# First attention of a two-layer kernel: every product on tiles of 64 rows and 32 columns

## The reference, cut to what matters

```python
qkv = zn @ w_qkv
qkv5 = qkv.reshape(b, n, H, HD, 3)
...
scores = jnp.einsum('bhqd,bhkd->bhqk', q, k) / SCALING
att = jax.nn.softmax(scores, axis=-1)
out = jnp.einsum('bhal,bhlv->bhav', att, v)
```

## Time and profile before

| | us |
|---|---|
| median of 3 runs | 1337.25 (1336.49 to 1337.75) |
| the profiled execution | 1338.72, span of its instructions 1336.7 |
| first attention, within the span | from 115.6 to about 780 |
| mean granted clock of TensorE | 0.955 |

### The profile page before, as it was taken

The page is one execution under the profiler, slowest core; times in us unless marked ns, Lnnn a source line. Parts: engine busy times, 40 slices in busy tenths (PEclk is TensorE's granted clock), DMA queues, the critical chain, the costliest instruction groups (busy, mean ns, idle before and its releaser), DMA issues. The chain is left out here.

```text
span 1336.7 us, 32111 instructions
## 1 busy us (share of the span) xinstructions
PE 1210.5 (91%) x13377; PEld 609.2 (46%) x13377; DVE 1007.4 (75%) x1288; ACT 837.6 (63%) x1447; POOL 238.0 (18%) x309
## 2 busy tenths in 40 slices
PE   6967999999999999999999978898899899899980
PEld 4641222232222223222322335555699566688870
DVE  6878999999999999999999547765675688533324
ACT  3543888888888888888888855565222466533331
POOL 4200110000000000000000011100573222145560
PEclk9986999999999999999999989998998699999995
DMA  5764133232233322323321121100010211223317
GB/s 146 200 206 91 30 65 75 45 78 62 61 79 75 76 59 63 81 45 74 68 51 75 57 69 44 39 17 16 19 44 28 68 37 37 60 72 99 101 50 191
DMA packets 75228, 95.35 MB, mean 71 GB/s; under 512 B 13236, under 2 KB 44684, under 8 KB 74052
## 3 DMA queue, kind: packets, MB, share of 16 engines
q1 hardware_dynamic: 69996, 83.19, 24.5%
q0 software_dynamic: 5088, 10.12, 2.5%
HBM read 54.30 MB, written 38.56 MB: 69 GB/s over the span
## 5 line engine op out<-in xcount | busy, mean ns | idle before, releaser
L613 DVE TENSOR_REDUCE b_mx<-psum 128x2 f32<-128x1024 f32 x507 | 595.6, 1218 | 38.8 <-PE psum L558 35.6
L671 ACT ACTIVATE b_exp_ring<-psum 128x512 f32<-128x512 f32 x1024 | 541.4, 600 | 131.2 <-PE psum L728 130.4
L728 PE MATMUL psum<-b_q,b_k 75*32 75x512 bf16 x4096 | 316.0, 384 | 1.3 <-ACT b_exp_ring L671 1.1
L702 PE MATMUL psum<-b_exp_ring,b_v 128*32 128x512 f32 x2048 | 266.6, 595 | 0.7 <-ACT b_exp_ring L671 0.7
L557 PE MATMUL psum<-b_k,b_q 64*128 64x512 bf16 x512 | 184.9, 396 | 29.3 <-DVE b_mx L613 11.9
L558 PE MATMUL psum<-b_ko,b_qo 64*128 64x512 bf16 x512 | 184.9, 396 | 0.0
L728 PEld LDWEIGHTS psum<-b_q,b_k 75*32 75x32 bf16 x4096 | 86.5, 95 | 177.1 <-ACT b_exp_ring L671 112.2
L557 PEld LDWEIGHTS psum<-b_k,b_q 64*128 64x128 bf16 x512 | 47.2, 93 | 231.4 <-issue 132.9
L745 POOL CAST b_neg<-b_neg_rest 16x128 bf16<-16x128 f32 x32 | 8.9, 279 | 609.5 <-DVE b_neg_rest L624 609.5
L1839 ACT ACTIVATE e_hT<-psum,e_b 128x358 f32<-128x358 f32 (+3 forms) x96 | 53.6, 559 | 75.4 <-PE psum L1859 72.0
L702 PEld LDWEIGHTS psum<-b_exp_ring,b_v 128*32 128x32 f32 x2048 | 60.4, 111 | 60.7 <-issue 14.5
(11 more groups left out here) (278 smaller groups left out, 1451.0 us busy)
## 6 DMA issues: line engine op xcount, KB each, us to landing
b_q<-q_ops SPq DMA_DIRECT2D x48, 192.0 KB
b_k<-k_ops SPq DMA_DIRECT2D x48, 192.0 KB
k_ops<-a_k SPq DMA_DIRECT2D x20, 256.0 KB, 3.1
x_disp<-b_zeros SPq DMA_DIRECT2D x13, 320.0 KB
e_x<-x_disp SPq DMA_DIRECT2D x8, 520.0 KB
v_ops<-a_vs SPq DMA_DIRECT2D x4, 1024.0 KB, 5.1
b_v<-v_ops SPq DMA_DIRECT2D x16, 256.0 KB
av_out<-b_acc SPq DMA_DIRECT2D x128, 32.0 KB, 1.7
```

The lines of the kernel that those rows point to most:

```text
L613: nc.vector.reduce_max(mx[:, d % 2, :, i // 2, i % 2], pair, AX.X).then_inc(sem("b_max_done"), 1)
L671: act.activation(ex[:, n % E_RING, :], g.bank(5 + n % 3), ACT.Exp, scale=ATT_SCALE)\
L702: last = nc.tensor.matmul(AV[32 * i:32 * i + 32, :], v[s][:, at_v:at_v + 32], ex[:, (4 * group + i) % E_RING, :], start=(kb == 0), stop=(k ...
L728: last = nc.tensor.matmul(g.bank(5 + n % 3)[keys, :], k[s][0:XROWS, h, kb * P + 32 * j:kb * P + 32 * j + 32], q[s][0:XROWS, h, half * BANK ...
```

## The change

All matmuls of the main loop but the transpose now use 64 rows and 32 columns. The nine products of a head are cut into eight (64 rows, tiles `q0`, `k0`) and a rest of 8 rows, which with the three rows of maxima and zeros against ones makes a second product of 64 rows (`qt`, `kt`). Head 0 of a duo lies on rows 0 to 63, head 1 on rows 64 to 127. A unit is `scores` and then `finished`, which adds the second product. Units 0 and 1 are of head 1, units 2 and 3 of head 0 (`HEADS`). Values are split by halves of the 128 keys: the lower half of block g - 2 is issued between the products of units 0 and 1, the upper half of block g - 1 between those of units 2 and 3, each in two chunks of 256 queries. Two semaphores, `b_upper` and `b_av`, hand bank 4 from one half to the other. The first item of a block comes behind its second unit, the others at its end. The evacuation comes behind the fifth exponential, the ring has 16 buffers, and maxima rows and loads are issued per head. The diff, cut to its core:

```diff
-E_RING = 12
+E_RING = 16
+HEADS = (1, 1, 0, 0)
...
-LOADS0 = 16 * (4 * NPART + 1)
+LOADS0 = 16 * (4 * NPART + 4 + 1)
...
     keep = lambda name, shape, dt=F32: g.tiles0.enter_context(nc.sbuf_tensor(name, shape, dt))
-    g.q0 = [keep(f"b_q{c}", [KROWS, HQ, T], BF16) for c in range(SLOTS)]
-    g.k0 = [keep(f"b_k{c}", [KROWS, HQ, T], BF16) for c in range(SLOTS)]
-    g.qo = [keep(f"b_qo{c}", [P, HQ // 2, T], BF16) for c in range(SLOTS)]
-    g.ko = [keep(f"b_ko{c}", [P, HQ // 2, T], BF16) for c in range(SLOTS)]
+    g.q0 = [keep(f"b_q{c}", [P, HQ // 2, T], BF16) for c in range(SLOTS)]
+    g.k0 = [keep(f"b_k{c}", [P, HQ // 2, T], BF16) for c in range(SLOTS)]
+    g.qt = [keep(f"b_qt{c}", [P, HQ // 2, T], BF16) for c in range(SLOTS)]
+    g.kt = [keep(f"b_kt{c}", [P, HQ // 2, T], BF16) for c in range(SLOTS)]
     g.v0 = [keep(f"b_v{c}", [P, HQ * P + 2 * HD]) for c in range(SLOTS)]
...
                     for c in range(SLOTS):
-                        nc.gpsimd.memset(g.k0[c][64:KROWS, :, :].rearrange("p h t -> p (h t)").bitcast(F32),
+                        nc.gpsimd.memset(g.kt[c][:, :, :].rearrange("p h t -> p (h t)").bitcast(F32),
                                          1.0 + 0x3F80 / 2 ** 23).then_inc(sem("b_ones"), 1)
-                        pool.wait_ge(sem("b_ones"), c + 1)
+                        nc.gpsimd.memset(g.qt[c][:, :, :].rearrange("p h t -> p (h t)").bitcast(F32), 0.0)\
+                          .then_inc(sem("b_ones"), 1)
+                        pool.wait_ge(sem("b_ones"), 2 * (c + 1))
...
         flat = "h i d t -> (i d) h t"
-        moved(g.q0[c][lo:lo + NPART * HD, :, :], g.q_ops[quad, :, :, :, :].rearrange(flat))
-        moved(g.k0[c][lo:lo + NPART * HD, :, :], g.k_ops[quad, :, m:m + NPART, :, :].rearrange(flat))
-        odd = slice(MROWS + lo, MROWS + lo + n * HD)
-        moved(g.qo[c][odd, :, :], g.q_ops[quad, 1:HQ:2, 0:n, :, :].rearrange(flat))
-        moved(g.ko[c][odd, :, :], g.k_ops[quad, 1:HQ:2, m:m + n, :, :].rearrange(flat))
+        for head in range(2):
+            rows = slice(MROWS * head + lo, MROWS * head + lo + n * HD)
+            moved(g.q0[c][rows, :, :], g.q_ops[quad, head:HQ:2, 0:n, :, :].rearrange(flat))
+            moved(g.k0[c][rows, :, :], g.k_ops[quad, head:HQ:2, m:m + n, :, :].rearrange(flat))
+            if n < NPART:
+                rest = slice(MROWS * head, MROWS * head + (NPART - n) * HD)
+                moved(g.qt[c][rest, :, :], g.q_ops[quad, head:HQ:2, n:NPART, :, :].rearrange(flat))
+                moved(g.kt[c][rest, :, :], g.k_ops[quad, head:HQ:2, m + n:m + NPART, :, :].rearrange(flat))
 FIRST = 5
-def maxima_scores(g, q, k, qo, ko, n, p, i):
-    t, keys = slice(i // 2 * P, i // 2 * P + P), slice(i % 2 * BANK, i % 2 * BANK + BANK)
-    g.nc.tensor.matmul(g.bank(2 * (n % 2)), q[0:MROWS, 2 * p, t], k[0:MROWS, 2 * p, keys], start=True, stop=True)
-    return g.nc.tensor.matmul(g.bank(2 * (n % 2) + 1), qo[MROWS:P, p, t], ko[MROWS:P, p, keys], start=True, stop=True)
+def head_rows(head):
+    return slice(MROWS * head, MROWS * head + MROWS)
+def maxima_scores(g, q, k, n, p, i):
+    keys = slice(i % 2 * BANK, i % 2 * BANK + BANK)
+    for head in range(2):
+        for j in range(STRIPS):
+            t = i // 2 * P + 32 * j
+            last = g.nc.tensor.matmul(g.bank(2 * (n % 2) + head)[32 * j:32 * j + 32, :], q[head_rows(head), p, t:t + 32],
+                                      k[head_rows(head), p, keys], start=True, stop=True)
+    return last
...
                        .then_inc(sem("b_exp_done"), 1)
-                    if u == 3 and d:
+                    if u == 4 and d:
                         evacuate(d - 1)
...
                     return
-                maxima_scores(g, q[s], k[s], qo[s], ko[s], n, p, i).then_inc(sem("b_max_scores"), 1)
-            def times_v(group):
+                maxima_scores(g, q[s], k[s], n, p, i).then_inc(sem("b_max_scores"), 1)
+            def unit(n):
+                d, kb, u = n // (4 * TB), n // 4 % TB, n % 4
+                return d // 2 % SLOTS, d % 2, kb, HEADS[u], u % 2
+            def products(n, ql, kl, first):
+                s, p, kb, head, half = unit(n)
+                for j in range(STRIPS):
+                    keys = slice(kb * P + 32 * j, kb * P + 32 * j + 32)
+                    last = nc.tensor.matmul(g.bank(5 + n % 3)[32 * j:32 * j + 32, :], kl[s][head_rows(head), p, keys],
+                                            ql[s][head_rows(head), p, half * BANK:(half + 1) * BANK],
+                                            start=first, stop=not first)
+                return last
+            def scores(n):
+                if n >= 3:
+                    pe.wait_ge(sem("b_exp_done"), n - 2)
+                products(n, q, k, True)
+            def finished(n):
+                products(n, qt, kt, False).then_inc(sem("b_scores"), 1)
+            def times_v(group, upper, c):
                 d, kb = group // TB, group % TB
                 s, p = d // 2 % SLOTS, d % 2
-                pe.wait_ge(sem("b_exp_done"), 4 * (group + 1))
-                if kb == 0 and d:
-                    pe.wait_ge(sem("b_acc"), d)
+                if upper and c == 0:
+                    pe.wait_ge(sem("b_exp_done"), 4 * (group + 1))
+                    if kb == 0 and d:
+                        pe.wait_ge(sem("b_acc"), d)
+                if c == 0:
+                    if not upper:
+                        pe.wait_ge(sem("b_upper"), group + 1)
+                    elif group:
+                        pe.wait_ge(sem("b_av"), group)
+                half, cols = head_rows(upper), slice(c * BANK // 2, (c + 1) * BANK // 2)
                 for i in range(4):
-                    at_v = (2 * p + i // 2) * P + kb * 2 * HD
-                    last = nc.tensor.matmul(AV[32 * i:32 * i + 32, :], v[s][:, at_v:at_v + 32],
-                                            ex[:, (4 * group + i) % E_RING, :], start=(kb == 0), stop=(kb == TB - 1))
-                last.then_inc(sem("b_av"), 1)
+                    at_v = (2 * p + HEADS[i]) * P + kb * 2 * HD
+                    last = nc.tensor.matmul(AV[32 * i:32 * i + 32, cols], v[s][half, at_v:at_v + 32],
+                                            ex[half, (4 * group + i) % E_RING, cols],
+                                            start=(kb == 0 and upper == 1 and c == 0),
+                                            stop=(kb == TB - 1 and upper == 0 and c == 1))
+                if c == 1:
+                    last.then_inc(sem("b_upper" if upper else "b_av"), 1)
...
             for d in range(DUOS):
-                s, p = d // 2 % SLOTS, d % 2
-                pe.wait_ge(sem("b_m_loaded"), 16 * NPART * (d + 1))
+                pe.wait_ge(sem("b_m_loaded"), 2 * 16 * NPART * (d + 1))
                 for kb in range(TB):
+                    group = TB * d + kb
+                    n, items = 4 * group, range(upto(d, kb - 1), upto(d, kb))
                     if d == DUOS - 1 and kb in PROJECT_AT:
                         project_piece(PROJECT_AT.index(kb))
-                    for i in range(4):
-                        n, h, half = 4 * (TB * d + kb) + i, 2 * p + i // 2, i % 2
-                        if n >= 3:
-                            pe.wait_ge(sem("b_exp_done"), n - 2)
-                        for j in range(STRIPS):
-                            keys = slice(32 * j, 32 * j + 32)
-                            last = nc.tensor.matmul(g.bank(5 + n % 3)[keys, :],
-                                                    k[s][0:XROWS, h, kb * P + 32 * j:kb * P + 32 * j + 32],
-                                                    q[s][0:XROWS, h, half * BANK:(half + 1) * BANK],
-                                                    start=True, stop=True)
-                        last.then_inc(sem("b_scores"), 1)
-                        if i == 2 and d + kb:
-                            times_v(TB * d + kb - 1)
-                    for n in range(upto(d, kb - 1), upto(d, kb)):
-                        item(n)
-            times_v(TB * DUOS - 1)
+                    for c in range(2):
+                        scores(n + c)
+                        if group >= 2:
+                            times_v(group - 2, 0, c)
+                        finished(n + c)
+                    for i in items[:1]:
+                        item(i)
+                    for c in range(2):
+                        scores(n + 2 + c)
+                        if group >= 1:
+                            times_v(group - 1, 1, c)
+                        finished(n + 2 + c)
+                    for i in items[1:]:
+                        item(i)
+            for group, upper in ((TB * DUOS - 2, 0), (TB * DUOS - 1, 1), (TB * DUOS - 1, 0)):
+                for c in range(2):
+                    times_v(group, upper, c)
...
                         sp.wait_ge(sem(("b_second", "b_third")[i - 1]), d + 1)
```

(20 more changed lines are left out.)

## The result

The change made the kernel slower: a median of 1358.7 us (1356.4 to 1364.5, four runs) against 1337.5 beside it, a ratio of 1.0165 (95% interval 1.0148 to 1.0183). The profiled execution took 1356.94 us with a span of 1355.2.

The account below looks back on a forecast made before the run. TensorE and VectorE, both nearly full, hold each other up. VectorE's floor of 19.1 us, with TensorE at 18.8 and 0.4 more, gave 19.5 per duo against 20.72: 37.2 gained less 2.5, so 1303 us (1281 to 1356).

Parts of the forecast that it names:

- (e): Bank 4's hand-over between value halves: 1.05 against 1.10 us due, upper bound +0.09 a half; taken at nothing.
- (h): Seventeen loads per quad for thirteen, memsets, ring buffers, store order: together nothing; ScalarE's 32 exponentials stay under 19 us.
- rival 5: Issue limits TensorE: 160 instructions a block at 14.8 ns, 19.0 a duo; with waits 19.9, 1315; chance inside the forecast's.
- (a): Maxima as eight matmuls of 64 rows, 32 columns: the 0.10 before and behind items goes, 1.6 us of TensorE per duo.
- (c): Values on 64 rows, 256 columns run beside scores on the other rows: unit and chunk 0.44 us, 17.6 per duo.
- rival 1: Row halves run one after the other: unit with its chunk 0.87 us for 0.44, 32.5 a duo, 1711; 12%.
- rival 4: Weight loads lie bare, 0.09 us each, two per unit: 6 us per duo, 24.9 a duo, 1474; 3%.
- rival 3: Engines go on holding each other up by 1.3 over the floor: 20.4, 1328 (9%); or 1337 stays (6%).
- Rival 2: Bank 4's hand-over costs its upper bound and more: 1.25 us per half block, 21.2 per duo, 1355; 12%.
- (f): ScalarE's evacuation of bank 4 comes after the fifth exponential: TensorE waits 0.75 us per duo for it.
- (g): Maxima rows by six small transfers instead of three, 3.5 us to issue, nothing to spare: 0.1 to 0.3 us per duo.
- (i): The end: last values in two halves after the last exponential, last unit later, blocks without items: +2.5 us.

Follow-up runs that it names:

- maxima_wide: The change with each maxima item again as two products of 64 rows by 128 columns; 1394.3 us.
- before_with_strips: The kernel before with only each maxima item as eight products of 64 rows by 32 columns, scores and values as before; 1347.9 us.
- late_split: The change with values in one 512-column chunk behind the first finishing products, waits swapped, three row transfers, GpSimd's megabyte in eight pieces; 1312.1 us.
- wait_order: The change with the wait for the lower half's end put before the wait for the exponentials, ahead of the upper half's values; 1337.9 us.
- hybrid_values: The change with swapped waits, three row transfers, lower half's values in one 512-column chunk, upper half's in two of 256; 1381.6 us.

## Why the prediction was wrong

The forecast was 1303 (1281 to 1356), faster at 0.67; 1358.7 is slower and just outside. The mechanisms it named are there; two terms that it set at nothing failed, the hand-over of bank 4 (e) and the transfers beside the instructions (h), and the supply of instructions was weighed in rival 5 alone, in a form that put it inside the forecast's range. For the profiled execution 1304.0 was forecast and 1356.9 measured. Of these 53 us some 23 are the undisturbed duo (20.23 for 19.5, 31 times), some 29 the disturbances (32, less some 3 that the duos of before had), 2.6 the end.

- **(a) right in kind, with a wrong reason.** The drains around the items are gone. maxima_wide's 2.0 us a duo is not the forecast's 1.6: its items stand alone, with two changes of shape each, where the kernel before had them in pairs. The text put the drain down to 32 against 128 columns; before_with_strips shows that rows count as well.
- **(b), (c) right.** A unit with its chunk takes 0.43 to 0.44, mixed types and all. So rival 1 fell, and rival 4: finishing products start 0.22 behind scores on the same rows (589.69, 589.91), the time that the scores stream, so their loads are hidden. On the load rule of the Trainium skill ("TensorE: Matmul & The Clock Gate", Part 3) the trace again decides against it, by these 0.22.
- **(d) right**: the two blocks that the transpose lengthens hold together 0.44 more than two plain ones, less the shorter last block (0.22 + 0.29 - 0.07); 0.42 forecast.
- **(e) failed.** "I take nothing ... the other one, for the exponentials, is met long before." The hand-over cost 0.19 a block, 0.10 a half, its stated upper bound (0.09). That the exponentials are long done did not help: their wait still stood behind the semaphore of bank 4 on TensorE's queue and had to be passed, 0.08 of the 0.19, as the swap shows. (late_split, where VectorE is the bound, has 2.30 a block, so little more than that was there to be won.) TensorE's own sum with it is 8 x 2.39 + 0.67 + 0.44 = 20.2, the measured duo; the forecast's 18.8 lacked 1.5. So rival 3 fell: no mutual waits are needed to make up the duo. Rival 2 had the mechanism of (e), with a price above it. With the measured block its own sum gives 20.3 a duo and 1327 (8 x 2.39 and 1.17), so it is chance that its 1355 lies near 1358.7.
- **(f) right**: 3.07 - 2.39 = 0.67 a duo, 0.75 forecast.
- **(g) right in size**: 7.4 us over 31 duos are 0.24 each (0.1 to 0.3 forecast), though they fall on nine duos. SP's six issues take 4.05, not 3.5.
- **(h) failed.** No product waits for the loads of a quad, but instruction packets do: some 12 us went when the loads were left out. Before, a packet lasted over 10 us of TensorE's time (450 loads and products in 20.72) and could come late. (h) also has a sum wrong: 32 x 0.60 is 19.2, not under 19; nothing came of it.
- **Rival 5 had the right place and the wrong form.** It took the density of instructions, 14.8 ns each, for a rate, 19.0 a duo, on top of which the waits of (f) come: 19.9, 1315. (19.0 and 0.75 are 19.75; the rest it does not name.) What binds is the chain of a packet: the next 256 must arrive within the time of the present 256. Where gap follows gap they took 3.97 us at the median (15.5 ns each, 20.0 a duo), at the least 3.43, and a late packet stops the engine whole, 0.3 to 5 us at a time. The Trainium skill, "Runtime: NRT & Kernel Launch", "Instruction fetch mechanics", says that the next page is fetched during the present one, and that the cost of crossing a boundary is mostly hidden. The trace agrees with the first: packets start 1.2 us behind a boundary and land 1.2 us or more ahead of the first instruction of the next. It does not agree with the second: 21.5 us in 29 boundaries with 160 instructions a block, 92.7 in 120 with 192, and 0.9 at most with 128.
- **(i) undersized**: +5.1 for +2.5. Three trailing half-groups run behind the last unit, and the blocks of the last duo without items also carry the hand-over.

Where the forecast's own mechanism is left alone (late_split), the duo is 19.70 against its 19.5, and VectorE is the bound: from 200 to 700 us it is busy 484.7 of 500, 97%.

## What to carry to other kernels

Smaller tiles are more instructions: count what TensorE gets for the span of a block of keys, and compare the time of 256 of them with the 3.4 to 4 us in which the next 256 came here. At 4.0 us (the change) late packets stopped the engine; at 4.9 (late_split) none did. Where two waits stand ahead of an instruction, put the one that ends last first in the program (0.08 us a block here). And a long product whose result is not wanted soon goes behind the short ones that another engine waits for, not ahead of them: that alone, with one chunk, was worth 51 us (1364.5 to 1313.7).

## What the runs showed that was not expected

- The supply of instructions can stop TensorE for 0.3 to 5 us at a fixed place in every 256 instructions, and a transfer of 1 MB beside it makes the longest stop; split into eight pieces it left 0.4 and 0.7 us in two blocks.
- Behind the 5 us pause TensorE was granted half its clock (0.50, 1.2 GHz) and then 0.64 on the mean, before it had 1.00 again, so that the pause cost more than its length: its block took 9.23 us, 6.5 over an undisturbed one (2.68), with a pause of 5.0. The windows (us; busy time of PE, PEld, DVE, ACT, POOL; granted clock; DMA share; GB/s):

```profile
425.90:430.90 5.00, 0.42 (x12) 0.00 (x0) 2.36 (x2) 0.51 (x2) 0.27 (x1) 0.75 0.44 99
430.90:433.00 2.10, 2.09 (x36) 1.02 (x41) 0.00 (x0) 0.64 (x2) 0.00 (x0) 0.50 0.00 0
433.00:436.00 3.00, 3.00 (x76) 1.76 (x76) 1.79 (x2) 1.86 (x4) 0.00 (x0) 0.64 0.03 5
436.00:439.30 3.30, 3.30 (x116) 1.94 (x108) 3.15 (x4) 2.93 (x6) 0.00 (x0) 1.00 0.02 5
```

- Open: why wait_order, with quicker blocks, has fewer gaps than the change (12 to 29, in one execution of each), and why hybrid_values is slower than either of its halves' kinds.
